# Ranks ahead of the weighing's second part, output transposes ahead of the value projection, both normalisations between two halves of the line terms

## The chip, the cores and the metric

The kernel runs on one core of one Trainium2 chip. The metric is the device time in microseconds of one execution. "Before" is the kernel as it stands, "after" the kernel with the change.

## The reference

The input `x` has 16 sequences ("batches" below, numbered 0 to 15) of 512 tokens and 128 features. The first layer is causal attention with 16 heads. Queries and keys are Pluecker lines: from two projected points of four coordinates each, six differences of products `p1[i] * p2[j] - p1[j] * p2[i]`, divided by their norm. The second layer is a mixture of experts: one shared expert and 8 routed ones, of which each token takes the 2 with the highest sigmoid score.

```python
q = _plucker_lines(bg @ W1_q.T, bg @ W2_q.T)      # bg: the token and the one before it
k = _plucker_lines(x @ W1_k.T, x @ W2_k.T)
attn = softmax(causal(q @ (k @ J6.T).T / sqrt(6)))
x = layernorm(x + (attn @ (x @ Wv.T + bv)) @ Wo.T + bo)
scores, idx = top_k(sigmoid(x @ Wr.T + rb), 2)
x = layernorm(x + shared(x) + sum over the 8 experts of cw[e] * expert_e(x))
```

## The kernel before

The program has two phases. The first, up to about 560 us, goes through the 16 batches. The second runs the experts and the last layer norm. Every engine has its own instruction stream, written out by hand; semaphores are the only ties between them. The body of one batch is written once for each engine. Batches 0 to 3 are peeled, batches 4 to 13 run in a loop over pairs, and batches 14 and 15 are peeled again.

In batch b each engine works on several batches at once:

- PE makes the scores (`logits(g, c)`, L727): four groups g of four heads, each in five chunks c of 1024 columns, into two PSUM tiles S that alternate. `weigh(b, par, g, blocks)` (L742) multiplies the masked probabilities of a group with the values. It is called in two parts, block 0 and blocks 1 to 3. Group 3 of batch b-1 is weighed in batch b, between `logits(0, 2)` and `logits(0, 4)`.
- For the next batch b+1 PE projects the points (`project_points`, L676 and L678) and the values (`project_values`, L686), and transposes the features (L700) late in batch b.
- For batch b-1 PE transposes the weighed values back to tokens (`transpose_out`, L766, two halves), transposes again (`transpose_o`, L773) and projects (L779). For batch b-2 it transposes and makes the router's logits (L812), for batch b-3 the ranks of the tokens in their experts (`ranks`, L825 and L830).
- ACT takes the exponentials (L1069, one for each chunk), and copies from PSUM: the points (L1054), the values (L1060), the weighed sums (L1076), the transposed output (L1081). It also issues the loads of the input, `load_columns` and `load_x`.
- POOL masks the diagonal blocks of the probabilities (L554), seven instructions for each group of heads: one each for chunks 0, 1 and 4, two each for chunks 2 and 3. `weigh` of a group waits for all seven. POOL also makes half of the products of the lines (`line_products`, L542, six instructions), the inverse standard deviation (L546), and sends rows of batch b-3 or b-4 to their experts by indirect DMA (L267, two for each quarter of a batch).
- DVE picks the two experts (`choose` of batch b-3, L1387 to L1405), normalises the layer's output of batch b-2 (`norm_out`, L1357), makes the other six products (`line_terms`, L1271), reads the ranks (`slots`, L1414 to L1422), divides the weighed values by their sums (`normalise`, L1330 and L1331, two halves), and goes on with the lines: `subtract_terms` (L1276), `square_lines` (L1279), `sum_squares` (L1282), norms and features.

Two PSUM tiles, W0 and W1, are shared by all the small products of PE. W1 takes the ranks and then half 0 of `transpose_out`, which therefore waits until `slots` has read the ranks (`rank_read`, raised by L1416). W0 takes the values and then half 1 of `transpose_out`, which waits for the copy of the values (`val_read`). `transpose_o` also writes W0 and waits for both halves of `normalise` (`outT_read`).

The order in PE's body of a batch from 4 on, as far as it matters here: `logits(0, 2)`, weigh group 3 block 0, `logits(0, 3)`, weigh group 3 blocks 1 to 3, `logits(0, 4)`, ranks, values, `logits(1, 0)`, transpose half 0, `logits(1, 1)`, transpose half 1, `logits(1, 2)`, weigh group 0 block 0, and so on.

## Time and profile before

| | |
|---|---|
| Time before, median of 3 runs | 969.52 us (966.25, 969.52, 973.77) |
| The profiled execution's own time | 962.28 us |
| Its span, first to last instruction | 960.5 us |
| Mean granted TensorE clock | 0.887 of full |
| Busy share of the span: PE, DVE, ACT, POOL | 76%, 64%, 59%, 61% |

The span of the profiled execution is 1.8 us shorter than its own time. All times below are in microseconds from the start of the span. The stretches of the first group of rows run from one copy of the values (L1060) to the next; the one from 265.71 starts in batch 7. Each busy share is an average over both phases. In the timeline views a row is a run of like instructions: start, length, engine, line, operation, output and inputs, count, and in square brackets the time that the engine sat idle before it and what ended that wait. Neighbouring instructions overlap a little, since one is started before the last has drained.

### The profile page before, as it was taken

What the parts mean: (1) busy time and instruction counts of PE and PEld (TensorE: products, weight loads), DVE (VectorE), ACT (ScalarE), POOL (GpSimd) and SP (SyncE); (2) the same over time, 40 slices, a digit from 0 to 9 for tenths busy, and PEclk for the clock granted to TensorE, in tenths of its full rate; (3) what the DMA queues carried; (4) which work ended last, traced back from release to release, by engine and by line L of the source; (5) the groups of instructions that cost most, each with busy time, mean ns of one, the idle gap of its engine ahead of it and who ended that gap; (6) DMA issues with size and microseconds to landing.
All of it is one profiled execution on the core that took longest, in us unless ns stands there. A gap on an engine that the chain in (4) does not pass through costs nothing.

```text
span 960.5 us, 22767 instructions
## 1 busy us (share of the span) xinstructions
PE 734.7 (76%) x7168; PEld 447.9 (47%) x7168; DVE 618.6 (64%) x1580; ACT 564.7 (59%) x875; POOL 590.7 (61%) x901
## 2 busy tenths in 40 slices
PE   2799997988988998898888777677766776758700
PEld 2444444434434444444443356565655555646600
DVE  7638888897788777977877367733333343333585
ACT  1488867667766867677777744334444454444436
POOL 3456667678768878778887744234454555444465
PEclk8599979899989989899999889988899898898855
DMA  6001011011201111120101622348332334221387
GB/s 225 12 24 28 19 52 48 30 59 47 66 22 49 60 38 50 44 66 28 58 26 45 190 65 70 78 74 217 84 70 62 74 68 79 67 55 32 91 228 209
DMA packets 125914, 69.85 MB, mean 73 GB/s; under 512 B 62820, under 2 KB 114278, under 8 KB 125840
## 3 DMA queue, kind: packets, MB, share of 16 engines
q1 hardware_dynamic: 106576, 43.44, 17.9%
q0 software_dynamic: 8512, 17.06, 5.7%
q10 hardware_dynamic: 10752, 8.39, 2.9%
q8 instruction: 43, 0.70, 0.3%
q14 instruction: 31, 0.25, 0.1%
HBM read 29.25 MB, written 31.21 MB: 63 GB/s over the span
## 4 chain that ended last, share of the span: by engine, by line
PE 40%; DVE 15%; issue 14%; ACT 10%; POOL 7%; another core or an unknown queue 6%; SPq 5%; DMA 2%; ACTq 0%; POOLq 0%; DVEq 0%
PE O L742 13%; PE S L727 8%; PE S L918 7%; ACT probs L1069 4%; PE O L940 4%; PE W L700 3%; POOL probs L554 3%; DVE hid L1617 3%; ACT hid L1198 2%; POOL prodB L542 2%; DVE prodA L1271 2%; SPq L452 2%; DVE hid L1599 1%; PE W L766 1%
## 5 line engine op out<-in xcount | busy, mean ns | idle before, releaser
L1069 ACT ACTIVATE probs<-S 128x1024 f32<-128x1024 f32 x320 | 319.7, 1043 | 149.5 <-PE S L727 125.5
L554 POOL TENSOR_SCALAR_AFFINE_SELECT probs<-probs 128x256 f32<-128x256 f32 (+1 forms) x448 | 218.1, 517 | 123.3 <-ACT probs L1069 122.7
L633 POOL DMA_INDIRECT z_scratch<-y,tails x136 | 133.9, 985 | 156.5 <-ACT y L1171 124.3
L742 PE MATMUL O<-probs,v_aug 128*32 128x512 f32 (+3 forms) x2048 | 187.5, 489 | 21.7 <-POOL probs L554 21.7
L1617 DVE TENSOR_TENSOR hid<-hid 128x512 f16<-128x512 f32 x100 | 70.6, 706 | 183.8 <-ACT hid L1198 157.3
L1179 ACT ACTIVATE silu<-S 128x512 f32<-128x512 f32 x100 | 59.9, 599 | 181.1 <-PE S L918 97.8
L940 PE MATMUL O<-w_T,hid 128*128 (+1 forms) x1200 | 102.4, 237 | 83.6 <-DVE hid L1617 67.8
L267 POOL DMA_INDIRECT rows_scratch<-xrow,slot_i x128 | 132.4, 1034 | 47.5 <-issue 29.6
L727 PE MATMUL S<-qkT 32*128 32x512 f16 (+3 forms) x1024 | 139.9, 317 | 20.0 <-ACT probs L1069 9.1
L940 PEld LDWEIGHTS O<-w_T,hid 128*128 128x128 f16 x1200 | 84.1, 106 | 105.6 <-issue 86.0
L918 PE MATMUL S<-xT_rt,w_T 128*128 128x256 f16 (+1 forms) x864 | 117.8, 289 | 7.8 <-issue 4.5
L742 PEld LDWEIGHTS O<-probs,v_aug 128*32 128x32 f32 x2048 | 57.3, 117 | 97.7 <-issue 78.6
L727 PEld LDWEIGHTS S<-qkT 32*128 32x128 f16 x1024 | 38.9, 93 | 123.3 <-issue 43.4
L918 PEld LDWEIGHTS S<-xT_rt,w_T 128*128 x864 | 83.9, 106 | 26.7 <-issue 12.2
L1198 ACT CAST hid<-hid 128x512 f16<-128x512 f32 x100 | 61.2, 612 | 12.8 <-DVE hid L1599 10.7
L1599 DVE SCALAR_TENSOR_TENSOR hid<-silu,S 128x512 f32<-128x512 f32 x100 | 68.0, 680 | 0.0
L1320 DVE COPY qkT<-W 128x1024 f16<-128x1024 f16 x64 | 44.2, 691 | 26.0 <-PE W L700 24.5
L918 PE MATMUL S<-xT_sh,w_T 128*128 128x256 f16 x384 | 53.2, 292 | 3.7 <-issue 3.6
L700 PE MATMUL W<-ident,feat 128*128 128x128 f16 x512 | 41.0, 226 | 12.8 <-DVE feat L1315 12.7
L542 POOL TENSOR_TENSOR prodB<-p 128x192 f32<-128x192 f32 (+2 forms) x96 | 49.8, 552 | 0.3 <-ACT p L1054 0.3
L700 PEld LDWEIGHTS W<-ident,feat 128*128 128x128 f16 x512 | 31.2, 100 | 36.9 <-issue 29.4
L676 PE MATMUL W<-w_allT,xT 128*128 128x256 f32 x128 | 44.1, 428 | 5.3 <-DVE w_allT L1246 5.3
(155 smaller groups left out, 989.6 us busy)
## 6 DMA issues: line engine op xcount, KB each, us to landing
z<-z_scratch SPq DMA_DIRECT2D x32, 256.0 KB, 4.2
xT<-in_x_cols ACTq DMA_DIRECT2D x16, 256.0 KB, 2.8
x_in<-in_L_attn_x ACTq DMA_DIRECT2D x16, 256.0 KB
x_scratch<-x SPq DMA_DIRECT2D x16, 256.0 KB, 2.6
x1T_scratch<-x1T SPq DMA_DIRECT2D x16, 256.0 KB
xT_sh<-x1T_scratch SPq DMA_DIRECT2D x16, 256.0 KB
x_in<-x_scratch SPq DMA_DIRECT2D x16, 256.0 KB
out<-res SPq DMA_DIRECT2D x16, 256.0 KB, 4.2
```

The source lines that it names most:

```text
L267: pool.indirect_dma_start(out=rows_dram, in_=xrow[:, par, t, k, :], in_offset=None, out_offset=bass.IndirectOffsetOnAxis(ap=slot_i[:, par, ...
L554: pool.affine_select(out=v, in_=v, compare_op=ALU.is_ge, fill=0.0, base=0, pattern=[[0, v.shape[1]], [1, P]], channel_multiplier=-1).then_ ...
L633: pool.indirect_dma_start(out=z_dram, in_=y[:, q, a, :], in_offset=None, out_offset=bass.IndirectOffsetOnAxis(ap=tails[:, q, a, 1:2].bitca ...
L700: mm = pe.transpose(w[:, s, t * P:(t + 1) * P], feat[:, first:first + 4, :].rearrange("p h f -> p (h f)"), ident16[:, :])
L727: mm = pe.matmul(S[(g + c) % 2][:, col:col + T - kb * P], k, q, start=True, stop=True)
L742: mm = pe.matmul(O[g // 2][32 * j:32 * j + 32, kb * P:T], value_weights(par, kb, g, j), probs[:, g % 2, c, col:col + T - kb * P], start=(g ...
L918: mm = pe.matmul(S[r % 2][:, k * UNIT + cols.start:k * UNIT + cols.stop], weights(e_of, w, k), xT[:, a, cols], start=(n == 0), stop=(n == 2))
L940: mm = pe.matmul(O[par][:, a * P:(a + 1) * P], hid16[:, par, h, k * UNIT + a * P:k * UNIT + (a + 1) * P], weights(e[a] if isinstance(e, tu ...
L1069: act.activation(probs[:, g % 2, c, :], S[(g + c) % 2][:, :], ACT.Exp, scale=-SCALE / SPLIT_UP ** 2).then_inc(s_exp, 1)
L1198: act.copy(hid16[:, r % 2, 0, :], hid[:, r % 2, :]).then_inc(hi_done, 1)
L1599: dve.scalar_tensor_tensor(out=hid[:, par, :], in0=silu[:, par, :], scalar=H_UP / UP ** 2, in1=S[par][:, 2 * UNIT:4 * UNIT], op0=ALU.mult, ...
L1617: dve.tensor_tensor(hid16[:, par, 1, :], hid[:, par, :], hid16[:, par, 0, :], ALU.subtract)\
```

## The change

PE: `ranks(b - 3)` moves from behind `logits(0, 4)` to ahead of the second part of the weighing of group 3. The two halves of `transpose_out` move up to either side of `logits(1, 0)`, and `project_values(b + 1)` moves behind `logits(1, 1)`. Since the order of the writers of W0 is turned round, `project_values` gets a wait for both halves of `normalise` of batch b-1, half 1 of `transpose_out` loses its wait for `val_read`, and `transpose_o` gets one.

ACT: the copy of the values moves from ahead of the exponentials of group 1 to behind its chunk 2. `load_x` moves from the start of the batch to behind the exponentials of group 0.

DVE: `line_terms` is cut in two calls of three products. The first stays, the second comes behind `slots` and both halves of `normalise`; `subtract_terms` and `square_lines` follow it.

```diff
             def project_values(c, par):
                 pe.wait_ge(pts_read, 2 * (c + 1))
+                if not (isinstance(c, int) and c < 2):
+                    pe.wait_ge(outT_read, 2 * (c - 1))
...
                     elif not (isinstance(c, int) and c < 2):
                         pe.wait_ge(rank_read, c)
-                elif after:
-                    pe.wait_ge(val_read, c + 3)
-                else:
+                elif not after:
...
             def transpose_o(c):
                 pe.wait_ge(outT_read, 2 * (c + 1))
+                pe.wait_ge(val_read, c + 3 if not (isinstance(c, int) and c + 3 > NB) else NB)
...
                 logits(0, 3)
+                if sends(b):
+                    ranks(b - 3)
                 if not first:
                     weigh(b - 1, 1 - par, 3, (1, 2, 3))
                 logits(0, 4)
-                if sends(b):
-                    ranks(b - 3)
+                if not first:
+                    transpose_out(b - 1, 0, not last)
+                logits(1, 0)
+                if not first:
+                    transpose_out(b - 1, 1, not last)
+                logits(1, 1)
                 if not last:
                     project_values(b + 1, 1 - par)
-                logits(1, 0)
-                if not first:
-                    transpose_out(b - 1, 0, not last)
-                logits(1, 1)
-                if not first:
-                    transpose_out(b - 1, 1, not last)
                 logits(1, 2)
...
                 if ahead(b):
                     load_columns(b + 2, par)
-                    load_x(b + 2, par)
...
                 exps(b, 0, (4,))
+                if ahead(b):
+                    load_x(b + 2, par)
+                exps(b, 1, (0, 1, 2))
                 if not last:
                     copy_values(b + 1, 1 - par)
-                exps(b, 1, range(NCHUNK))
+                exps(b, 1, (3, 4))
...
+            def line_terms(c, part=None):
+
+                if part != 1:
+                    dve.wait_ge(pts_read, 2 * (c + 1))
+                for k, (dst, many, one) in enumerate(products(prodA, 1, 0)):
+                    if part is None or k // 3 == part:
+                        ins = dve.tensor_tensor(dst, many, one, ALU.mult)
+                if part != 0:
+                    chain(ins)
...
                 if not last:
-                    line_terms(b + 1)
+                    line_terms(b + 1, 0)
                 if sends(b):
                     slots(b - 3, 1 - par)
-
                 if not first:
                     normalise(b - 1, 0)
-                if not last:
-                    subtract_terms(b + 1)
-                if not last:
-                    square_lines()
-                if not first:
                     normalise(b - 1, 1)
                 if not last:
+                    line_terms(b + 1, 1)
+                    subtract_terms(b + 1)
+                    square_lines()
                     sum_squares()
```

## Rows read from the trace of the kernel before

**Rows 1.** Stretches: length, busy PE, PEld, DVE, ACT, POOL (instructions), granted clock, DMA share, GB/s.

```profile
70.85:98.85 28.00, 26.70 (x272) 13.43 (x270) 22.53 (x48) 23.90 (x29) 20.68 (x38) 1.00 0.11 30
...
265.71:300.86 35.15, 30.46 (x297) 15.18 (x295) 28.51 (x78) 24.07 (x29) 25.51 (x44) 0.90 0.14 45
300.86:332.81 31.95, 29.17 (x297) 14.77 (x295) 24.79 (x72) 23.76 (x29) 25.78 (x44) 0.95 0.15 50
```

**Rows 2.** Timeline of PE in batch 6.

```profile
230.46 1.50 PE L742 MATMUL O<-probs,v_aug 128*32 128x384 f32 x24
...
232.52 0.24 PE L830 MATMUL W<-picks,ones 128*128 128x32 f16 x4
232.62 1.14 PE L686 MATMUL W<-w_allT,xT 128*128 128x128 f32 x8
...
234.91 0.66 PE L766 MATMUL W<-ident,oT_raw 128*128 128x128 f32 x4
...
238.13 1.94 PE L742 MATMUL O<-probs,v_aug 128*32 128x512 f32 x8 [2.24 <-POOL probs L554]
```

**Rows 3.** Timeline of POOL in batch 6, narrow windows.

```profile
230.29 0.98 POOL L554 TENSOR_SCALAR_AFFINE_SELECT probs<-probs 128x256 f32<-128x256 f32 x1
...
231.60 2.93 POOL L542 TENSOR_TENSOR prodB<-p 128x192 f32<-128x192 f32 x6
...
235.57 1.12 POOL L554 TENSOR_SCALAR_AFFINE_SELECT probs<-probs 128x256 f32<-128x256 f32 x1
...
236.65 1.35 POOL L554 TENSOR_SCALAR_AFFINE_SELECT probs<-probs 128x512 f32<-128x512 f32 x1
```

**Rows 4.** Timeline of DVE in batch 6.

```profile
227.90 0.23 DVE L1398 TENSOR_TENSOR picks<-one 128x32 f16<-128x32 f32 x1
...
229.61 1.40 DVE L1271 TENSOR_TENSOR prodA<-p 128x192 f32<-128x192 f32 x6
232.87 0.19 DVE L1414 TENSOR_TENSOR rt_slot<-W,next_slot 128x32 f32<-128x32 f32 x1 [1.86 <-PE W L830]
...
233.45 0.55 DVE L1419 TENSOR_TENSOR oneslot<-one,rt_slot 128x32 f32<-128x32 f32 x1
...
234.70 0.36 DVE L1330 RECIPROCAL rden<-W 128x32 f32<-128x32 f32 x1
235.09 0.42 DVE L1331 TENSOR_TENSOR o_tok<-W,rden 128x256 f32<-128x256 f32 x1
235.43 0.99 DVE L1276 TENSOR_TENSOR prodA<-prodA,prodB 128x768 f32<-128x768 f32 x1
236.46 1.04 DVE L1279 TENSOR_TENSOR prodB<-prodA 128x768 f32<-128x768 f32 x1
```

**Rows 5.** Timelines of DVE, POOL and PE in batch 7.

```profile
261.80 6.92 DVE L1271 TENSOR_TENSOR prodA<-p 128x192 f32<-128x192 f32 x6
...
262.47 1.10 DVE L1271 TENSOR_TENSOR prodA<-p 128x64 f32<-128x64 f32 x1
...
266.39 2.58 POOL L554 TENSOR_SCALAR_AFFINE_SELECT probs<-probs 128x256 f32<-128x256 f32 x6
...
269.28 1.08 PE L766 MATMUL W<-ident,oT_raw 128*128 128x128 f32 x4 [3.29 <-DVE next_slot L1416]
...
272.42 1.94 PE L742 MATMUL O<-probs,v_aug 128*32 128x512 f32 x8
```

**Rows 6.** Single instruction of DVE and next wait of PE, batch 4.

```profile
159.00 5.53 DVE L1405 TENSOR_SCALAR place_i<-place_i 128x8 int32<-128x8 int32 x1
...
167.59 1.08 PE L766 MATMUL W<-ident,oT_raw 128*128 128x128 f32 x4 [5.23 <-DVE next_slot L1416]
```

**Rows 7.** ACT's copies in batch 6: weighed sums, then values.

```profile
232.03 0.59 ACT L1076 COPY oT_raw<-O 128x512 f32<-128x512 f32 x1 [0.26 <-PE O L742]
...
233.79 0.63 ACT L1060 COPY v_aug<-W 128x512 f32<-128x512 f32 x1 [0.18 <-PE W L686]
```

**Rows 8.** PE in batch 1, weighing of group 0.

```profile
73.17 1.07 PE L742 MATMUL O<-probs,v_aug 128*32 128x512 f32 x8 [0.22 <-POOL probs L554]
```

More of the change, by code:

```diff
@@ L1265, in small_constants @@
                                          op1=ALU.subtract)
-            def line_terms(c):
-                dve.wait_ge(pts_read, 2 * (c + 1))
-                for dst, many, one in products(prodA, 1, 0):
-                    ins = dve.tensor_tensor(dst, many, one, ALU.mult)
-                chain(ins)
+            def line_terms(c, part=None):
[6 more added lines that the diff above has]
+                    chain(ins)
             def subtract_terms(c):
```

## The prediction

> **What bounds the kernel now.** I read the page first: no engine is over 76% busy and PE heads the chain of waits, so what matters is where PE stops. Then I cut the first phase into stretches between two copies of the values [rows 1]. Batch 1, which routes nothing yet, takes 28.00 us at a granted clock of 1.00. Batches 7 and 8 take 35.15 and 31.95 us at 0.90 and 0.95. The instruction counts on PE differ only a little, so the 4 to 7 us more are waits and the lower clock behind them. From batch 5 to 14 there are two kinds of batch.
>
> The common kind is batch 6; 8, 9, 10, 12, 13 and 14 look like it. PE has done everything ahead of `weigh` of group 0 and stands 2.24 us for POOL's last mask [rows 2]. (The seven such waits run from 2.24 to 2.55 us.) POOL is busy all the time from the end of the batch before, so its own chain sets the moment. In that chain three masks are too long [rows 3]: 0.98, 1.12 and 1.35 us. Unhindered, six masks in a row take 2.58 us [rows 5], which is 0.4 us for a narrow one and some 0.7 for the wide one of chunk 4. Beside the first long one DVE runs its six line products from 229.61 to 231.0, beside the other two it subtracts and squares, from 235.43 to 237.5 [rows 4]. Each blocked mask ends about 0.25 us behind a DVE instruction. The hindrance is 0.58 + 0.72 + 0.65 = 1.95 us.
>
> The other kind is batch 7, with 5 and 11 like it (PE waits of 3.28, 3.29 and 3.30 us). Here it is DVE that loses: its six line products take 6.92 us instead of 1.40 [rows 4, 5], while POOL's masks beside them run at full speed. `slots` comes behind them, the transposes of PE wait for it until 269.28, and group 0 is weighed at 272.42 [rows 5]. POOL had finished the masks of group 0 at about 268.5. I call this the lock-out. Batch 4 shows it earlier, in an update of eight numbers per partition that takes 5.53 us, and PE waits 5.23 us [rows 6] in front of the transposes; batch 3 has a mild one.
>
> **The common batch after the change.** I follow batch 6. *Ranks:* they move ahead of the second weighing part, which starts at 230.46 [rows 2]. The picks are there at 228.1 [rows 4] and the first copy of the points has long been read, so nothing waits; the part itself comes 0.15 us later, behind 0.24 us of rank products. The 1.86 us that DVE idles at `slots` [rows 4] goes. *Transposes:* half 0 needs the copy of the weighed sums, which ended at 232.6 [rows 7] and now ends at 232.8. The half takes 0.6 us, a chunk of scores between the halves 0.3, so the halves end at 233.4 and 234.3, half 1 0.3 us after a chunk and 1.2 us sooner than now (234.91 + 0.66) [rows 2]. *Normalise:* 0.36 + 0.42 us with some overlap [rows 4], so half 1 is done at 235.2. *The added wait:* the values now stand behind that. PE has finished `logits(1, 1)` at 234.65, idles some 0.65 us, spends 1.14 on the values [rows 2] and 0.3 on `logits(1, 2)`, and is ready for group 0 at 236.75, 0.9 us later than now (238.13 - 2.24 = 235.9). Queued behind the wait are exactly these two and the weighing. It is hidden as long as POOL is later. *POOL:* only three products stand beside the first mask now, and they are over at 230.35; 0.58 us comes back, and the products of the lines end at 234.0 in place of 234.5 [rows 3]. The five masks behind them would end at 236.1 unhindered. But DVE starts its second three products at 235.2 and subtracts from 236.0, so at least the wide mask is hindered. That gives 236.6 if it slips in between the two, 238.2 if it and its predecessor are held behind both. With PE's 236.75 as a floor, weighing starts between 236.75 and 238.2: a gain of 1.4 to -0.1 us. I take 0.8, as the seams between DVE's instructions did let masks in before [rows 3, 4]. Seven batches: **-5.6** (-10 to +0.7).
>
> On this point a rule of the Trainium skill speaks against the change. The row shows that POOL's mask took 1.12 us beside a subtraction of two operands and that masks beside `normalise`, whose product reads PSUM and one SBUF operand, were not slowed. The skill (Advanced Engine Details and Errata, GPSIMD Details) says that the Pool engine shares a read and a write interface with DVE and conflicts with DVE instructions that have two SBUF inputs. Line products have two: moved into the masks, they would hold up those in place of the one they held up before. By the rule alone the common batch would gain nothing; it is the second rival.
>
> **The locked-out batches.** In batch 7 everything lies 31.92 us later than in 6 (265.71 in [rows 1] less 233.79 in [rows 7]). Three of the six products are ahead of `slots` now. In the trace the third ended at 263.6 (262.47 + 1.10, [rows 5]), and from there `slots` needs 0.4 us to release the transposes, against 264.7 when PE wants them. So the 3.29 us wait is gone. PE is ready at 236.75 + 31.92 = 268.7, POOL at 268.5 or a little later: 272.42 - 268.7 = 3.7, less 0.3 for what the second three may still hold up. Three batches: **-10.2** (-11 to 0, the latter if the lock-out goes on in `slots`).
>
> **Batches 3 and 4.** DVE is last there. Three products less ahead of `slots` are worth half of 1.40 us [rows 4], 0.7 each: **-1.4** (-3 to 0).
>
> **Batches 1 and 2.** There are no ranks, and PE waits only 0.22 us for the masks [rows 8]. The 0.9 us by which PE is later has next to no cover: **+1.6** (0 to +2).
>
> **Clock.** In a common batch 0.95 over 31.95 us [rows 1] means 3.2 us at 1.2 GHz, all of it behind the 2.24 us stop; a locked-out batch has twice that. Stops of 0.2, 0.65 and below 1 us in place of one of 2.24 should often leave the clock at 2.4 GHz, as in batch 1. If PE alone set the time, that would be 1.6 us; but behind the stop ACT's exponentials pace the batch as well, so I take 0.3 for each of the seven and 0.5 for each of the three: **-3.6** (-10 to 0).
>
> **The rest at nothing.** The copy of the values (0.63 us, [rows 7]) moves from in front of ACT's group 1 to a place where ACT waits for scores; its reader `transpose_o` comes 4 us later. `load_x` leaves the start of the batch, where ACT is not what PE waits for, and is issued while an exponential runs; the load is for a batch that is two ahead. In batch 0 it frees ACT earlier, but PE's point projections come last there. DVE's features end no later: normalise half 1 only changes places with subtract and square, and DVE idles before the router's logits anyway. In batch 15 nothing of the lines is left. The second phase follows the end of the first one to one.
>
> **Sum.** -5.6 - 10.2 - 1.4 + 1.6 - 3.6 = -19.2 us against the profiled execution's 962.3: 943.1. The median of the runs shown is 7.2 us above that execution (with more lock-outs, possibly, since they look like a matter of chance), so the same saving gives 950.3; I say **951**.
>
> **Rivals.**
> *The lock-out goes on (chance 0.22).* Behind the ranks `slots` makes two small products of two SBUF operands; in batch 6 the second took 0.55 us beside POOL's products [rows 4]. If they are locked out as the line products were, some 2 us each, `normalise` half 1 ends at about 270.2, the values wait for it, and weighing starts at 272.0: 0.4 us gained, not 3.7. For it: the row of batch 4 shows that a tiny instruction is hit as hard [rows 6]. Against: the locked-out instructions all followed another without a wait between, and here there are waits. Sum: -5.6 - 1.2 - 1.4 + 1.6 - 2 = -8.6: 961.
> *The terms hold up the masks (0.13).* Each common batch +0.1, a locked-out one -2.3, clock -1: +0.7 - 6.9 - 1.4 + 1.6 - 1 = -7: 962.5.
> *Slower (0.10).* The new wait ties PE to DVE in every batch. If the lock-out falls on `slots` or `normalise` in common batches too, each costs what separates the two kinds, 35.15 - 31.95 = 3.2 us [rows 1]. It decides from the third such batch on top of the first rival's sum; with six, -8.6 + 19 = +10.6: 980.
> *Nothing happens (0.05):* the masks end when they did and the lock-outs vanish for another reason: 969.
>
> **How the numbers follow.** The forecast has 0.50, its own range 944 to 959. No more than 0.2 may be left out: 944 to 970 leaves out the slower rival and the tail below. About 1% (9.7 us) is what a measurement of this kernel can tell from no change. The forecast lies beyond it nearly always (0.48), the first two rivals in a third of cases (0.12): faster 0.60; slower 0.07; within it 0.33.
>
> **What would show it.** Right: L1416 no longer ends waits of PE in the batches from 5 on; PE's wait for L554 falls from 2.24 to under 1 us; a wait of 0.5 to 0.8 us for `normalise` appears before L686; the mask at the start of a batch takes 0.4 us; granted clock nearer 1.00. Wrong: products at L1419 of 2 us, waits of 3 us before L686, masks of over 1 us at the old places.

## The result and the profile after

The change made the kernel slower: 1006.17 us in the median of 4 runs (1004.84 to 1010.39), against 969.86 us for the kernel before (966.25 to 973.77). The ratio of the runs is 1.038, with a 95% interval of 1.033 to 1.043. The forecast of 951 us, and its range, lie on the wrong side. Ratios and their intervals, here and below, leave out executions that the chip ran in a slower state (over 1.5% above the fastest of their kernel), so a ratio isn't always the quotient of the two medians, which are over all executions.

The profiled execution has a span of 1004.0 us, 43.5 more than before's. I split it at the first matmul of `weigh` of group 0 (L744 after, L742 before) of batches 0 and 15. The start is 2.4 us shorter (39.5 for 41.9), the fifteen batch periods between are 520.0 us for 489.0, and what follows is 444.6 us for 429.6. I don't count the last 15 us to the change: three kernels of the experiments, with the same code in that phase, took 429, 433 and 443 us there. That all 15 are chance isn't shown. The change owns the 31 us in the batches. The six periods from batch 8 to batch 14 alone hold 21.6 of them (218.7 us for 197.1).

Within the fifteen periods PE stands 24.9 us longer (75.6 us for 50.7) and is busy 6.0 us longer, with as many matmuls (4339), at a granted clock of 0.906 for 0.925.

First the stretches again, as in [rows 1]: from copy to copy of the values (now L1061), for batch 1, a batch of the better kind, and one of the worse:

```profile
core 0: us, PE busy (x) PEld busy (x) DVE busy (x) ACT busy (x) POOL busy (x), PEclk, DMA share, GB/s
72.55:101.17 28.62, 26.57 (x276) 13.51 (x274) 22.36 (x49) 23.89 (x30) 17.59 (x35) 1.00 0.10 29
207.11:239.45 32.34, 30.53 (x305) 15.00 (x299) 24.36 (x70) 24.09 (x31) 24.21 (x43) 0.92 0.16 50
347.41:384.20 36.79, 31.49 (x303) 15.72 (x295) 29.65 (x72) 24.08 (x30) 24.46 (x43) 0.87 0.14 43
```

DVE is the engine whose busy time grows, by 5.3 us for two more instructions, in the stretch that is 4.45 us longer. Next some of the waits of PE from 20 to 600 us (waiting instruction, who ended the wait, us in total, times, longest). Of before:

```profile
PE O L742 <- POOL probs L554: 21.7, 11, 2.6
PE W L766 <- DVE next_slot L1416: 17.5, 6, 5.2
```

and of after, the same view:

```profile
PE W L688 <- DVE o_tok L1337: 37.1, 14, 4.3
PE W L766 <- DVE next_slot L1422: 7.1, 2, 5.3
PE O L744 <- POOL probs L554: 3.3, 3, 1.7
```

The two waits that the forecast meant to shorten fell from 39.2 to 10.4 us, as it said. In their place stands the added one, of the values (L688) for `normalise` (L1337): 37.1 us where the forecast has 14 times 0.65, or 9. In the fifteen periods these three waits together grew by 9.8 us. Of the other 15 that PE stands longer, 8.0 are waits in the middle of a chunk of scores, which the view puts down to PE itself or outside the core's engines (11.6 us for 3.6). The eight of them over 0.8 us all stand behind a weighing of group 0 that took 1.42 to 1.94 us, which is all or partly at half clock, in place of 1.07. They come with the stops, then, though what makes them so long isn't shown. The rest are small: the copy of the weighed sums 2.8 us, the router's logits 2.3, the exponentials 1.3.

One batch shows where the 37.1 us come from. DVE, POOL and PE of after in batch 7 (start, length; L1420 to L1428 are `slots`, L1336 and L1337 `normalise`):

```profile
266.51 0.19 DVE L1420 TENSOR_TENSOR rt_slot<-W,next_slot 128x32 f32<-128x32 f32 x1 [0.63 <-PE W L831]
...
266.81 5.62 DVE L1425 TENSOR_TENSOR oneslot<-one,rt_slot 128x32 f32<-128x32 f32 x2
...
272.73 0.17 DVE L1428 CAST slot_i<-slot_f 128x8 int32<-128x8 f32 x1
...
273.95 0.43 DVE L1337 TENSOR_TENSOR o_tok<-W,rden 128x256 f32<-128x256 f32 x1
274.29 0.73 DVE L1276 TENSOR_TENSOR prodA<-p 128x64 f32<-128x64 f32 x3
```

POOL beside it, masks (L554) and line products (L542):

```profile
265.88 0.78 POOL L554 TENSOR_SCALAR_AFFINE_SELECT probs<-probs 128x256 f32<-128x256 f32 x2
266.62 2.93 POOL L542 TENSOR_TENSOR prodB<-p 128x192 f32<-128x192 f32 x6
269.51 2.77 POOL L554 TENSOR_SCALAR_AFFINE_SELECT probs<-probs 128x256 f32<-128x256 f32 x7
```

And PE, last half of the transposes, a chunk of scores, the values, and the weighing of group 0:

```profile
269.20 0.66 PE L766 MATMUL W<-ident,oT_raw 128*128 128x128 f32 x4
269.79 0.39 PE L729 MATMUL S<-qkT 32*128 32x512 f16 x2
274.52 2.05 PE L688 MATMUL W<-w_allT,xT 128*128 128x128 f32 x8 [4.34 <-DVE o_tok L1337]
...
277.04 1.94 PE L744 MATMUL O<-probs,v_aug 128*32 128x512 f32 x8
```

The ranks are read in time and the transposes end at 269.9. But the first of the two products of `slots`, 128x32 elements, stands 5.52 us. It ends at 272.33, and POOL's row of back-to-back work, which began at 265.88, ends at 272.28. `normalise` is behind it on DVE, the values behind that on PE. PE idles 4.34 us and comes back at half clock (1.2 GHz): the values take 2.05 us in place of 1.14 [rows 2]. `slots` and the values had nothing to do with each other before; now they stand in one line.

Batch 6 of after is one of the two batches from 5 to 14 (the other is 8) in which this doesn't happen. The same lines of DVE there:

```profile
232.59 1.00 DVE L1425 TENSOR_TENSOR oneslot<-one,rt_slot 128x32 f32<-128x32 f32 x2
...
236.46 0.42 DVE L1337 TENSOR_TENSOR o_tok<-W,rden 128x256 f32<-128x256 f32 x1
236.81 1.92 DVE L1276 TENSOR_TENSOR prodA<-p 128x64 f32<-128x64 f32 x3
```

POOL's masks ahead of and behind its products:

```profile
231.70 0.77 POOL L554 TENSOR_SCALAR_AFFINE_SELECT probs<-probs 128x256 f32<-128x256 f32 x2
...
235.33 2.78 POOL L554 TENSOR_SCALAR_AFFINE_SELECT probs<-probs 128x256 f32<-128x256 f32 x7
```

And PE, values and weighing:

```profile
237.03 1.13 PE L688 MATMUL W<-w_allT,xT 128*128 128x128 f32 x8 [0.68 <-DVE o_tok L1337]
...
238.42 1.07 PE L744 MATMUL O<-probs,v_aug 128*32 128x512 f32 x8
```

There the forecast held nearly to the tenth: 0.68 us of added wait (0.65 forecast), no wait for the masks, first mask 0.4 instead of 0.98, weighing at full clock. The second three line products now take 1.92 us instead of 0.7, beside masks that run unhindered: the conflict is paid by DVE here, where nothing waits for it.

### The profile page after: what moved, and what is told of

Its sections match the earlier page's. It is cut to its first block, busy times and chain, and to the rows that moved or that the text cites. A ratio compares the mean times of both kernels' runs of the same rounds, so it can differ in the third digit from the quotient of the medians.

```text
span 1004.0 us, 22783 instructions
## 1 busy us (share of the span) xinstructions
PE 744.8 (74%) x7168; PEld 459.1 (46%) x7168; DVE 648.8 (65%) x1580; ACT 566.2 (56%) x875; POOL 572.9 (57%) x901
## 4 chain that ended last, share of the span: by engine, by line
PE 46%; DVE 20%; issue 11%; ACT 10%; another core or an unknown queue 7%; SPq 3%; DMA 2%; POOL 1%; ACTq 0%; DVEq 0%; POOLq 0%
PE O L744 13%; PE S L919 9%; PE S L729 8%; PE O L941 4%; DVE oneslot L1425 4%; ACT probs L1070 4%; PE W L702 3%; DVE hid L1620 3%; ACT hid L1201 3%; PE W L676 2%; PE W L688 2%; DVE hid L1602 1%; ACT x1T L1087 1%; DVE stats L1671 1%
## 5 line engine op out<-in xcount | busy, mean ns | idle before, releaser
L554 POOL TENSOR_SCALAR_AFFINE_SELECT probs<-probs 128x256 f32<-128x256 f32 (+1 forms) x448 | 202.5, 481 | 169.4 <-ACT probs L1070 168.6
L744 PE MATMUL O<-probs,v_aug 128*32 128x512 f32 (+3 forms) x2048 | 184.4, 482 | 3.3 <-POOL probs L554 3.3
L919 PE MATMUL S<-xT_rt,w_T 128*128 128x256 f16 (+1 forms) x864 | 122.7, 298 | 8.4 <-DMA tails<-rows_scratch 5.3
L729 PEld LDWEIGHTS S<-qkT 32*128 32x128 f16 x1024 | 39.2, 93 | 133.5 <-ACT probs L1070 48.5
L919 PEld LDWEIGHTS S<-xT_rt,w_T 128*128 x864 | 87.1, 109 | 28.7 <-issue 11.7
L744 PEld LDWEIGHTS O<-probs,v_aug 128*32 128x32 f32 x2048 | 56.4, 115 | 74.2 <-issue 59.1
L688 PE MATMUL W<-w_allT,xT 128*128 128x128 f32 x128 | 28.9, 397 | 37.8 <-DVE o_tok L1337 37.1
L702 PEld LDWEIGHTS W<-ident,feat 128*128 128x128 f16 x512 | 31.2, 100 | 38.8 <-issue 27.6
L542 POOL TENSOR_TENSOR prodB<-p 128x192 f32<-128x192 f32 (+2 forms) x96 | 48.4, 538 | 0.6 <-ACT p L1055 0.6
```

What stands on the lines that cost most here:

```text
L554: pool.affine_select(out=v, in_=v, compare_op=ALU.is_ge, fill=0.0, base=0, pattern=[[0, v.shape[1]], [1, P]], channel_multiplier=-1).then_ ...
L702: mm = pe.transpose(w[:, s, t * P:(t + 1) * P], feat[:, first:first + 4, :].rearrange("p h f -> p (h f)"), ident16[:, :])
L729: mm = pe.matmul(S[(g + c) % 2][:, col:col + T - kb * P], k, q, start=True, stop=True)
L744: mm = pe.matmul(O[g // 2][32 * j:32 * j + 32, kb * P:T], value_weights(par, kb, g, j), probs[:, g % 2, c, col:col + T - kb * P], start=(g ...
L919: mm = pe.matmul(S[r % 2][:, k * UNIT + cols.start:k * UNIT + cols.stop], weights(e_of, w, k), xT[:, a, cols], start=(n == 0), stop=(n == 2))
```

## The experiments

Fifteen kernels, in four groups, with runs of the kernel before beside each group. Absolute times from different groups can't be compared: before had medians of 961.79, 882.64, 884.88 and 971.0 us in them (see the last section). "Free" and "locked" below are about batches 5 to 14: locked is a batch in which a DVE instruction ahead of `normalise` takes over 1 us more than usual beside POOL's row.

**One part alone.** First the split of the line terms with the new place of `normalise` alone (kernel before, DVE's part of the change), then PE's and ACT's part with the old order of DVE, then only the ranks moved up in the kernel before.

```diff
 e3_dve:     DVE body as after; PE and ACT as before
 e4_pe_act:  PE and ACT as after; DVE body as before
 e7_ranks, on before:
                 logits(0, 3)
+                if sends(b):
+                    ranks(b - 3)
                 if not first:
                     weigh(b - 1, 1 - par, 3, (1, 2, 3))
                 logits(0, 4)
-                if sends(b):
-                    ranks(b - 3)
```

> The kernel before with DVE's part of the change alone: three line products ahead of `slots`, both halves of `normalise`, then three more, subtract, square. PE and ACT have their old order, so ranks come 1.7 us later than in the changed kernel and the values wait for no `normalise`. Lock-out theory: `slots` waits for the ranks as before and its products fall in the middle of POOL's, where they took 0.35 and 0.55 us; few lock-outs, and PE doesn't pass them on: 950 to 972, the best of it from the mask at the start of a batch, which is hindered less. Rival (the split of the line terms is what costs: three of them now hold up the masks of group 0): PE waits more than 2.3 us for the masks, 975 or more.

> PE's and ACT's part of the change alone, DVE in its old order (six line products, `slots`, normalise, subtract, square, normalise). Theory of the first meeting: no lock-outs in common batches, but the values now wait for the second `normalise`, behind subtract and square: PE waits 2 to 2.5 us ahead of the values and hardly for the masks; a batch takes 0 to 1 us more than before, 962 to 980. Rival (PE's new order brings the lock-outs): products of `slots` of 5 us, 1000 and more.

> The kernel before with one edit: the ranks ahead of the second part of the weighing. Theory of the first meeting: six products stand ahead of `slots`, POOL's first mask waits, nothing is locked out in the common batches; the products of `slots` come some 1.7 us earlier, ahead of POOL's six; the transposes and PE's wait for the masks stay. 955 to 970, no difference from before that can be told. Rival (the early ranks are to blame): lock-outs in `slots`, which PE sees only through the second transposes and `transpose_o`: 975 or more.

DVE's part alone: 986.55 us, ratio 1.030 (1.022 to 1.037); missed. `slots` comes 2 us later here than after, and its products are still held in all ten batches. In seven of them the longer takes 3.3 to 4.0 us and ends with POOL's row or one mask before; in the other three one of them takes 2.1 us and ends 1.3 us before the row does. DVE in batch 6, where POOL first pauses, for under 0.1 us, at 238.43:

```profile
231.69 0.74 DVE L1273 TENSOR_TENSOR prodA<-p 128x192 f32<-128x192 f32 x3
234.88 0.19 DVE L1417 TENSOR_TENSOR rt_slot<-W,next_slot 128x32 f32<-128x32 f32 x1 [2.44 <-PE W L830]
...
235.19 3.40 DVE L1422 TENSOR_TENSOR oneslot<-one,rt_slot 128x32 f32<-128x32 f32 x2
```

So the split with the new place of `normalise` brings the lock-out of `slots` with PE's order as before. There is no added wait of the values here; what is late is the end of DVE's batch, and PE waits 24.4 us (13 times) for the rows that DVE cuts in two 16-bit parts for the router (`split`).

PE's and ACT's part alone: 928.99 us beside 882.64, ratio 1.050 (1.043 to 1.057), the worst of all. Seven of its ten batches are free, with products of 0.33 and 0.18 us. But half 1 of `normalise` stands behind `subtract_terms` and `square_lines`, and the values now wait for it: 40.6 us in 14 waits. The free batches take 33.9 to 35.1 us, against 32.1 to 33.4 in the trace of before: here the added wait costs without any lock-out, and more than the 0 to 1 us a batch that I had expected. The ranks alone: 881.75 us, 0.998 (0.994 to 1.003), no difference.

**The wait in `slots` taken away.** In the first kernel the sums are kept in PSUM, so that each product has one SBUF operand; in the second the products, their sum and the cast come behind both halves of `normalise`; in the third two unused reductions stand in front of the products, to let DVE ask later. In the first the ranks count as read only behind the products.

```diff
 e1_psum:
-                slot = rt["slot"][:, :, :]
+                slot = W1[:, 64:64 + NT * NE].rearrange("p (t e) -> p t e", t=NT)
...
+                dve.sem_inc(rank_read, 1)
 e2_late:
                 if sends(b):
-                    slots(b - 3, 1 - par)
+                    read_ranks(b - 3)
                 if not first:
                     normalise(b - 1, 0)
                     normalise(b - 1, 1)
+                if sends(b):
+                    place_picks(1 - par)
 e5_delay2:
+                for k in range(2):
+                    dve.tensor_reduce(idle_out[:, k], slot, AX.X, ALU.add)
                 for k in range(2):
                     ins = dve.tensor_tensor(oneslot[:, k], one[:, k], slot, ALU.mult)
```

> The changed kernel, but `slots` writes its sums into free columns of W1 in PSUM, so that the two products that follow (L1425 in the changed kernel) have one SBUF and one PSUM operand; the ranks are declared read only behind these products, some 0.5 us later. Lock-out theory (the products of two SBUF operands wait out POOL's whole run of work, 5.5 us, in 8 of 11 batches, and PE's new wait for `normalise` passes it on): both products take 0.2 us each, PE's waits of 3 to 4 us ahead of the values shrink to about 1 us, and the time falls by some 8 x 4.5 us to about 965 to 972. Order theory (the new place of the values behind `normalise` costs PE by itself, lock-out or not): the products get short, but the time stays above 990. Lock-out moves on (the rival in between): another DVE instruction of two SBUF operands, the second three line products, takes 2 to 5 us in its place; the time is 965 to 990, since nothing on PE waits for these.

> The changed kernel, but only the two instructions of `slots` that read the ranks stay in place; the two products, their sum and the cast come behind both halves of `normalise`, ahead of the second three line products. Lock-out theory: nothing that can be locked out stands ahead of `normalise`, so PE's wait ahead of the values is 0.7 to 1 us in every batch; the time falls to 955 to 970. The products may still be locked out at the new place, which PE doesn't see. Order theory: above 990. If POOL's dispatch suffers from the later slots (its first indirect DMA of a batch waits for the cast), there is a wait of POOL for L1428 or its successor, and the time lies between.

> The changed kernel with two short reductions (one SBUF operand each, some 0.1 to 0.2 us each) on DVE ahead of the two products of `slots`; their results are not used. In the changed kernel the first product was locked out where it came 0.14 to 0.19 us behind the start of POOL's first line product (eight batches) and not where it came 0.33 us behind (two batches). Phase theory: later by 0.2 to 0.3 us it comes at 0.35 to 0.5 us and is locked out in three batches at most; the time falls to below 985 though there is more work on DVE. If the place (ahead of POOL's six products) is what counts and not the moment, it is locked out in eight batches again, and the time is 1006 or more.

All three beside 961.79 us. With the sums in PSUM: 991.51 us, ratio 1.030 (1.022 to 1.037). The products now never take more than 0.2 us. In seven batches the cast two instructions on takes 4.9 us instead, and ends with POOL's row, as they had (DVE in batch 8):

```profile
308.95 0.28 DVE L1424 TENSOR_TENSOR oneslot<-one,W 128x32 f32<-128x32 f32 x2
309.38 0.22 DVE L1427 TENSOR_REDUCE slot_f<-oneslot 128x8 f32<-128x64 f32 x1 [0.15 <-DVE oneslot L1424]
309.63 4.92 DVE L1428 CAST slot_i<-slot_f 128x8 int32<-128x8 f32 x1
314.46 0.34 DVE L1336 RECIPROCAL rden<-W 128x32 f32<-128x32 f32 x1
```

It has one SBUF operand of 8 elements per partition. The reduction of `slots` (0.22 us), the sums that read PSUM (0.16 to 0.20) and `normalise` (up to 0.36 and 0.43) take no longer in any batch of any run. The time is above 990, where the order theory had it, but not for its reason: the hold moved on, to the next instruction that could be held.

With the products late: 974.55 us, 1.017 (1.012 to 1.022). The wait of the values is 9.3 us in 14 (longest 0.7), as the forecast had it, and the periods from batch 5 on are 31.4 to 33.2 us. Set beside the 1.038 of the first runs, from another group, that puts the lock-out in front of `normalise` at about half of the loss. Some of the rest moves: PE now waits 11.9 us, in 8 waits, for `split`. But the traced run is the fastest of the five (962.6 us), and its fifteen periods are 487.5 us, less than before's 489.0; what the others lost isn't in a trace. With the two reductions: 992.52 us, 1.034 (1.028 to 1.041). Eight batches are still locked, three with 5.4 us and five with 1.9 and 2.1. I had thought that the moment of DVE's request, 0.14 to 0.19 us behind POOL's first product, was what decided; that theory fell.

**The split undone, and its time filled.** What was left in common to all that were locked was that three line products stood where six had been. So the split is undone and nothing else; in the second kernel it stays, and three more products into an unused 16-bit array stand behind the first three, so that DVE does more work than after but is as busy as before at that place.

```diff
 e6_nosplit, e12_nosplit:
-                    line_terms(b + 1, 0)
+                    line_terms(b + 1)
...
-                    line_terms(b + 1, 1)
 e10_twice, in line_terms:
+                if part == 0:
+                    for k, (dst, many, one) in enumerate(products(prodA, 1, 0)):
+                        if k // 3 == 1:
+                            l0, n = ((0, 1), (1, 2), (3, 3))[k - 3]
+                            dve.tensor_tensor(unused[:, :, l0:l0 + n], many, one, ALU.mult)
```

> The changed kernel with all six line products of DVE ahead of `slots` again; PE, ACT and the two `normalise` side by side as in the change. Theory of the first meeting, formed from the runs so far: where the six products are still running when POOL begins its row of work, POOL's first mask waits (0.91 to 0.98 us, all seven common batches of the kernel before) and no product of `slots` is locked out behind it; where only three stand there, POOL begins unhindered (0.41 to 0.43 us) and a later instruction of DVE with two SBUF operands, or a cast, waits out POOL's row (29 of 33 batches). So here the first mask takes over 0.9 us in about seven batches, the products of `slots` 0.2 to 0.6 us there, and the time is 955 to 975. Rival (the early ranks put the products of `slots` at the start of POOL's six products, and that is what counts): locked out for 5 us as in the changed kernel, time near 1000.

> The changed kernel with three more products ahead of `slots`: the second three line products are made there as well, into an array that nothing reads, and again at their new place. Everything behind them is as in the changed kernel; DVE has 0.6 us more work in each batch. Theory of the first meeting: POOL's first mask waits for them (over 0.9 us), the lock-outs of 5.5 us behind it go, and the time falls below 980 though there is more work. Rival (the moment or the order counts): lock-outs stay in eight batches and the time is 1006 to 1015.

890.63 and 894.63 us, beside 882.64 (quotients of the medians 1.009 and 1.014, without an interval, so they settle nothing about the time). Both have seven free batches of ten, and most of the free ones take 30.4 to 31.7 us, against 32.1 to 33.4 in the trace of before. In the one with the unused products the first mask takes 0.63 to 0.73 us and the products of `slots` 0.18 and 0.63. More work on DVE, and no lock-out in `slots`: it is not the amount of it.

Since the level of the times changes from group to group, the changed kernel, the one without the split and two variants of it were run together:

```diff
 e11_after:          no edit
 e13_nosplit_psum:   e12_nosplit with the sums in PSUM (as e1_psum)
 e14_nosplit_late:   e12_nosplit with the products late (as e2_late)
```

> The changed kernel once more, unedited, beside the three that follow, so that they share one chip and one set of runs of the kernel before. Expected: ratio 1.03 to 1.05, slots' first product 5 us or more in most batches from 4 on, weighing of group 0 every 36 to 37 us there. If the ratio is below 1.02 here, the loss depends on the chip, and the ratios of experiments from different chips can't be set beside each other.

> The changed kernel with all six line products in front of slots, where the kernel before had them, and nothing else undone. Theory of the first meeting (the mask that starts while DVE's products still run waits, and then nobody is locked out): products of slots 0.2 to 0.5 us in some 7 of 11 batches, first mask 0.9 to 1.0 us there, ratio to the kernel before 0.99 to 1.02, ratio to the changed kernel 0.96 to 0.98. Rival (the changed order of PE, with values behind normalise, is what costs): still 1.03 or more.

> As the one without the split, and the sums of slots are kept in PSUM so that its two products read one operand there (rank_read is raised behind the products). Theory of the first meeting: nothing more to win in the undisturbed batches, and in those where the six products themselves are locked out the products of slots no longer lose another 2 us each; the cast behind them can, though. Ratio to the kernel before 0.98 to 1.01. Rival (a locked-out batch costs what it costs before slots is reached): same as without this edit.

> As the one without the split, and slots' two products, sum and cast stand behind both halves of normalise, so that between DVE's line products and normalise nothing is left with two SBUF operands. If the wait of PE for normalise is what a locked-out batch costs, it falls to under 0.7 us in all batches but those in which the six line products are themselves locked out: ratio to the kernel before 0.975 to 1.0. Rival (the late cast delays the rows' way to the experts and the next features, as in the run with the split and late products): 1.00 to 1.02.

Beside 884.88 us: the changed kernel 904.77 us, 1.022 (1.015 to 1.029); without the split 894.15, 1.012 (1.007 to 1.017); with PSUM 900.89, 1.013 (1.003 to 1.024); with late products 903.05, 1.012 (1.003 to 1.022). The changed kernel's loss is smaller here than at first, though eight batches of ten are locked again: only three of them with the full 5.7 to 6.0 us, five with holds of some 2 us. Its fifteen periods are 505.6 us, where they were 520.0 in its first trace. The interval of the version without the split only just overlaps the changed kernel's, and its median is 10.6 us lower. In its free batches PE does what I had forecast of the change, though POOL's first mask takes its 0.9 to 1.0 us again. PE in batch 10:

```profile
373.76 0.63 PE L766 MATMUL W<-ident,oT_raw 128*128 128x128 f32 x4 [0.31 <-ACT oT_raw L1077]
...
376.29 1.13 PE L688 MATMUL W<-w_allT,xT 128*128 128x128 f32 x8 [0.68 <-DVE o_tok L1337]
...
378.86 1.07 PE L744 MATMUL O<-probs,v_aug 128*32 128x512 f32 x8 [1.11 <-POOL probs L554]
```

Of the four expectations only the version without the split kept to its range beside before (0.99 to 1.02); beside the changed kernel it is at 0.988, where I had 0.96 to 0.98. The changed kernel lost less than its 1.03 to 1.05. The two variants came to 1.013 and 1.012, where I had at most 1.01 and 1.00.

Four periods of the version without the split are 30.7 to 30.9 us. It is still not faster than before. Its four locked batches take 35.8 to 37.4 us, where before's three took 34.3 to 34.6 in the first trace (there is none of before in this group). The late products can't help there, as the line products themselves are held; five batches fell to that in that run.

**What ends a lock-out, and what the values' wait costs.** Two kernels keep W0's old order (values, then half 1 of the transposes), so that the values don't wait for `normalise`, with ranks and half 0 moved up. The last takes three products from POOL's row: it leaves them out in every batch but the first, so its lines of the keys are wrong.

```diff
 e15_half0, on e7_ranks:
                 logits(0, 4)
+                if not first:
+                    transpose_out(b - 1, 0, not last)
                 if not last:
                     project_values(b + 1, 1 - par)
                 logits(1, 0)
-                if not first:
-                    transpose_out(b - 1, 0, not last)
 e17_half0_norm: the same, and DVE's body as in e12_nosplit
 e16_pool3, on after:
-                for dst, many, one in products(prodB, 0, 1):
-                    pool.tensor_tensor(dst, many, one, ALU.mult).then_inc(prodB_done, 1)
+                for k, (dst, many, one) in enumerate(products(prodB, 0, 1)):
+                    if isinstance(c, int) and c == 0 or k < 3:
+                        pool.tensor_tensor(dst, many, one, ALU.mult).then_inc(
+                            prodB_done, 1 if isinstance(c, int) and c == 0 or k < 2 else 4)
```

> The kernel before with the ranks ahead of the second weighing part and half 0 of the output transposes ahead of the values; DVE, ACT and the values' place relative to half 1 as before, so no wait of PE for normalise. If that wait is what the version without the split loses again: 0.985 to 0.997 of before, the common batch 31 to 32 us. Rival (there was nothing to win on PE, since the masks of POOL or the exponentials end the batch): 0.997 to 1.005.

> As the one before it, and both halves of normalise ahead of subtract and square. The first masks behind POOL's products should then not meet them: 0.3 to 0.7 us less per common batch than without it, ratio 0.98 to 0.995. Rival (half 1 comes so late that DVE idles in front of it and the features come later): 1.00 to 1.01.

> The changed kernel, with three of POOL's six line products left out for every batch but the first, so that the lines of the keys are wrong and POOL's row of back-to-back work is 1.6 us shorter (0.43 + 0.51 + 0.63). If a locked-out instruction waits for the end of POOL's row, the first product of slots takes 3.8 to 4.1 us instead of 5.5 where it took that. If it is a fixed time or a count of its own, it takes 5.5 again. If the masks now have to wait for exponentials between them, POOL's row breaks earlier, and the product ends there.

Beside 971.0 us: 983.14, 1.015 (1.009 to 1.021), and 989.53, 1.021 (1.015 to 1.028). Both missed. The wait of the values for `normalise` is gone and nothing is won. In the trace of the first nine batches of ten are free, and the fifteen periods are 490.8 us, no shorter than before's 489.0 with seven: eight of its free batches take 31.2 to 33.4 us and one 35.6, with a wait of 2.0 us that the trace puts outside the core's engines. All have waits for POOL's masks of 1.5 to 1.8 us, and a new one of 0.4 us of half 1 for the copy of the values. What follows the batches takes 442.7 us. There is no trace of before from this group, so why its runs are 12 us above before's I can't say.

The shortened row, in a single run: 969.91 us beside 971.0. POOL's row in batch 11:

```profile
389.20 1.50 POOL L543 TENSOR_TENSOR prodB<-p 128x192 f32<-128x192 f32 x3
390.65 2.07 POOL L556 TENSOR_SCALAR_AFFINE_SELECT probs<-probs 128x256 f32<-128x256 f32 x5
393.07 0.41 POOL L556 TENSOR_SCALAR_AFFINE_SELECT probs<-probs 128x256 f32<-128x256 f32 x1 [0.35 <-ACT probs L1072]
```

and DVE's two products beside it, with the reduction behind them:

```profile
389.37 3.50 DVE L1427 TENSOR_TENSOR oneslot<-one,rt_slot 128x32 f32<-128x32 f32 x2
392.90 0.22 DVE L1429 TENSOR_REDUCE slot_f<-oneslot 128x8 f32<-128x64 f32 x1
```

The first product takes 3.39 us instead of 5.5 and is over at 392.77; POOL's row broke at 392.72, for want of an exponential. Two more batches have 3.36 and 3.43. In two others it took 2.78 and 2.84 and slipped through one mask before the row's end. I had expected 3.8 to 4.1, with an unbroken row. So this long hold has no length of its own: it lasts until POOL stops, or one mask less. The remaining three locked batches show another kind: there the first product takes 2.28 us and ends 0.9 us before the row, and the second takes 1.02.

**Two kinds of hold.** In the shorter kind, DVE is slow from the second line product on (0.5 us for 0.32, then 1.1 for 0.27), and each of the next two products takes some 1.9 to 2.5 us while POOL's row goes on. All three locked batches of before are of it, and batch 11 of after, where POOL's row runs from 408.75 to 415.31:

```profile
408.01 1.76 DVE L1276 TENSOR_TENSOR prodA<-p 128x192 f32<-128x192 f32 x3
...
409.98 4.08 DVE L1425 TENSOR_TENSOR oneslot<-one,rt_slot 128x32 f32<-128x32 f32 x2
```

The long kind, one small instruction held to the end of the row, is in the other seven locked batches of after and in none from 5 on of before. Of the eight locked batches each of e5 and e11, five and four are of the shorter kind.

**All together.** The first mask behind POOL's last transfer, against what is held on DVE, in batches 5 to 14 of each trace:

| | first mask 0.6 us or more, DVE free | DVE held |
|---|---|---|
| six products at that place: before, e4, e6, e7, e12, e13, e14, e15, e17 | 59 of 90 | 31, in the line products (in 3 of them in `slots` too) |
| three, and three unused (e10) | 7 of 10 | 3, in the unused ones |
| three: after, e1, e3, e5, e11, e16 | none | 49 of 60, in `slots`; in the other 11 neither |
| three, and the products of `slots` behind `normalise`: e2 | none | none ahead of `normalise`; those late products take 1.4 to 1.7 us in 8 of 10 |

## Why the prediction was wrong

**What bounds the kernel.** Right, as far as it went: the two waits named are the two that shrank. It missed that the long first mask of a common batch, which I had counted as 0.58 us to be had, is the state in which DVE is free. Where POOL's first mask meets the later line products, it waits for them (0.9 to 1.0 us) and DVE then passes. In the changed kernel that mask takes 0.41 to 0.43 us in every batch from 5 on, and `slots` is held in eight of ten. Over all runs, with three products at that place the first mask was never held and `slots` was in 49 batches of 60; with six, `slots` was held in 3 of 90. That the two go together is shown, how the hardware comes to it is not.

**Common batch, -5.6.** The term's own steps were right where the batch stayed free: added wait 0.68 for 0.65, weighing ready at 237.0 for 236.75 on before's clock (238.48 less the shift of 1.5 us), first mask 0.41. That is two batches in ten. The step that failed is "half 1 is done at 235.2": it has `normalise` follow on the transposes and puts what `slots` can add ahead of it at nothing, since `slots` was read as it stood in batch 6, 0.35 and 0.55 us. In seven batches of the changed kernel its first product took 5.52 to 5.58 us, in one its two took 2.05 and 2.10. In batch 7 half 1 of `normalise` is done at 274.4, which is 238.8 with the starts of POOL's rows (265.88 and 230.29) laid on each other, 3.6 us later than forecast.

**Locked-out batches, -10.2.** This is where the sum broke. "From there `slots` needs 0.4 us to release the transposes" held: L1422 ended waits of 7.1 us for 17.5. "So the 3.29 us wait is gone" did not: it went one step down, to L688 ([rows 5] against the rows of batch 7 above), and grew to 4.34, since the first product is held nearly from the beginning of POOL's row to its end. The six periods from batch 8 to batch 14 are 3.6 us longer each, where I had five common ones shorter by 0.8 and one locked-out one by 3.4.

**The rivals.** "The lock-out goes on" was the mechanism, and "Slower" its reach: the values tied to DVE and locked out in common batches too. My ground against it, that the held instructions all followed another without a wait, was read from four cases [rows 5, 6]; the product in question follows one without a wait as well, I looked only at `slots` as a whole. And I priced it at some 2 us each from the line products, where the 5.53 us of eight numbers [rows 6] was the nearer row: a small instruction can be held as long as POOL's row lasts. With 4.5 us, about what the stop (4.34 for 0.68) and the values at half clock (2.05 for 1.13) cost in the batches shown, for each of eight batches, in place of 3.2 for six, the rival would have given -8.6 + 36 on top of 969.5, or 997 us.

**The rule on the shared interface** (Advanced Engine Details and Errata, GPSIMD Details, in the Trainium skill) pointed at the right pair of engines, and I weighed it for the wrong sufferer. I let it lengthen POOL's masks by some tenths; the trace shows the other side of it, DVE's product of two SBUF inputs held 5.5 us. The run with the sums in PSUM agrees that one SBUF operand less frees the products (0.2 us). The cast of 4.92 us, with one SBUF input, agrees only if it is one of the instructions in a 2-port mode that the rule names too, which no run here tells.

**Batches 1 and 2, +1.6.** Measured 0.7 and 0.9: right. **Batches 3 and 4, -1.4:** +0.4 and +0.1, so this term failed too; in batch 4 `place_i`, which is ahead of all that moved, was held 4.95 us again. **Clock, -3.6:** it went the other way in locked batches, 0.87 for the 0.90 or 0.95 of [rows 1]. **The rest at nothing:** the copy of the values and `load_x` show no wait of their own.

Left open: why three products in place of six change who is served first, and what makes the first kind of hold or the second; whether the 15 us behind the batches in the first pair of traces are chance alone; and why the early half 0 (e15) loses.

## What to carry to other kernels

Where two engines hinder each other, a delay of some tenths on one may be what keeps the other from a stop of many us: before taking it away, look which batches show the delay and which the stop, and expect the price from the longest hold in the trace, not from the shortest. Before letting a matmul wait for an engine that can be held, list every instruction ahead on that engine that could be the one held, small ones first. And cost a change that moves a wait one engine further by its bad case times the number of batches.

## What the hardware did that I had not expected

- A DVE product of 128x32 took 0.18 us alone and up to 6.0 beside a row of POOL's; a cast of 8 elements per partition 4.92; the reduction of `slots` (0.22 us) and what read PSUM (0.16 to 0.42) were not held. POOL, when it was the one to wait, lost 0.2 to 0.6 us.
- The clock that PE gets behind a stop doesn't follow from its length: in e15 the weighing behind 1.56 us of waiting took 1.94 us and behind 1.60 us 1.07, and in before it took 1.94 behind 2.24 and 1.06 behind 2.25. A term for the clock worked out from single stops is a guess.
- The phase behind the batches took 429 to 445 us in the traces of the first pair and of two groups of runs, and 356 to 361 in those of the other two, whatever the kernel. Two groups were on the same chip, with 961.79 and 884.88 us for before, so the chip alone doesn't decide it. Where it took 429 us or more, the silu (L1179 before) waits for something that the trace puts outside the core's engines, 62.8 us from 600 to 850 in before, 29 to 58 in the others; where it took 361 or less, it has no such wait. What it is I don't know. The trace of the changed kernel was 96.5 us shorter the second time (907.5 for 1004.0), 84.6 of them in this phase, so only ratios within one group say anything.
